# Mask, maximum and shift of a tile's attention scores: one vector operation each over 1024 elements of two PSUM banks instead of two of 512

## The reference, cut to what matters

```python
x = x + attn(cond(x, ...), W_attn, b_attn, W_proj, b_proj)
x = x + ffn(gru(cond_2048, x, W_ih, W_hh, b_ih, b_hh), weight, scale_weight, bias)

# inside attn: 32 heads of width 8, 32 tokens
scores = jnp.einsum('bhqd,bhkd->bhqk', q, k) / jnp.sqrt(jnp.float32(D))
scores = jnp.where(causal, scores, jnp.float32(MASKED_BIAS))
scores = scores + alibi * m
probs = jax.nn.softmax(scores, axis=-1)
attn = jnp.einsum('bhqk,bhkd->bhqd', probs, v)
```

## Time and profile before

| | us |
|---|---|
| median of 3 runs | 511.05 (510.9 to 513.89) |
| span of the profiled execution, first to last instruction | 509.6 |
| PE busy / PEld busy | 472.8 / 426.2 |
| DVE busy | 359.8 |
| ACT busy | 242.5 |
| POOL busy | 49.6 |
| attention, start-up included | about 0 to 318 |
| GRU and output | about 318 to 509.6 |

### The profile page before, as it was taken

How to read it: one execution, slowest core, us unless ns; L and a number is a source line. 1 busy time by engine, 2 the same in 40 slices (tenths; PEclk the granted TensorE clock), 3 DMA queues, 4 the chain that set the end, 5 groups by cost and what they waited for, 6 DMA issues and landing times.

```text
span 509.6 us, 14167 instructions
## 1 busy us (share of the span) xinstructions
PE 472.8 (93%) x5310; PEld 426.2 (84%) x5310; DVE 359.8 (71%) x1049; ACT 242.5 (48%) x584; POOL 49.6 (10%) x67
## 2 busy tenths in 40 slices
PE   8489899999999999999989887799999999999993
PEld 5258698888897888888878776799999999999993
DVE  3814789697897896987876786356666677676665
ACT  1252554746556648365566443434444444444441
POOL 7321201201203012012020000000000000000000
PEclk9969999999999999999999999989999999999998
DMA  8525543443544534444443420000000000100001
GB/s 304 205 59 148 151 115 84 146 117 109 149 103 118 153 94 144 113 113 106 99 109 76 113 67 1 1 1 30 34 21 21 21 21 21 39 23 21 22 21 41
DMA packets 81596, 42.45 MB, mean 83 GB/s; under 512 B 53792, under 2 KB 74400, under 8 KB 81568
## 3 DMA queue, kind: packets, MB, share of 16 engines
q1 hardware_dynamic: 81568, 42.07, 28.9%
HBM read 25.28 MB, written 16.78 MB: 83 GB/s over the span
## 4 chain that ended last, share of the span: by engine, by line
PE 69%; DVE 11%; ACT 5%; issue 5%; POOL 3%; POOLq 0%; DVEq 0%; ACTq 0%
PE ps_s L1071 7%; PE ps_t L1083 6%; PE ps_s L1234 6%; PE ps_t L1234 6%; PE ps_o L1234 6%; PE ps_a L1034 5%; PE ps_t L1212 5%; PE ps_a L1212 5%; PE ps_m L1212 4%; PE ps_s L1212 4%; PE ps_m L1112 4%; PE ps_a L1025 4%; DVE mx L761 3%; PE ps_a L1000 3%; POOL yT_r L432 3%
## 5 line engine op out<-in xcount | busy, mean ns | idle before, releaser
L1071 PE MATMUL ps_s<-kbd,qbd 128*128 128x128 f32 x512 | 65.7, 282 | 0.0
L515 ACT ACTIVATE sc<-sc 128x512 f32<-128x512 f32 x64 | 38.8, 628 | 53.7 <-DVE sc L765 53.7
L753 DVE COPY_PREDICATED masked<-kst,ps_s 128x512 f32<-128x512 int32 x64 | 46.7, 739 | 24.3 <-issue 19.9
L1071 PEld LDWEIGHTS ps_s<-kbd,qbd 128*128 128x128 f32 x512 | 62.9, 196 | 0.1
L1025 PE MATMUL ps_a<-yT_r,w_qkv_r 128*128 128x512 f32 x192 | 52.9, 420 | 2.6 <-ACT yT_r L478 1.5
L1025 PEld LDWEIGHTS ps_a<-yT_r,w_qkv_r 128*128 128x128 f32 x192 | 35.6, 196 | 14.3 <-POOL yT_r L432 4.9
L896 DVE SCALAR_TENSOR_TENSOR rg<-ps_o,vec,rg 128x128 f32<-128x128 f32 x64 | 19.5, 346 | 35.3 <-PE ps_o L1234 28.5
L765 DVE TENSOR_TENSOR sc<-masked,mx 128x512 f32<-128x512 f32 x64 | 41.0, 681 | 0.0
L761 DVE TENSOR_REDUCE mx<-masked 128x16 f32<-128x512 f32 x64 | 40.4, 671 | 0.0
L1083 PE MATMUL ps_t<-kst,sc 128*128 128x128 f32 x256 | 35.2, 277 | 4.6 <-ACT sc L515 4.6
L788 DVE SCALAR_TENSOR_TENSOR xf<-ps_m,b_out,xf 128x128 f32 (+1 forms) x64 | 24.9, 435 | 19.1 <-PE ps_m L1112 19.0
(11 more groups left out here) (105 smaller groups left out, 874.6 us busy)
## 6 DMA issues: line engine op xcount, KB each, us to landing
xf<-in_x_feat SPq DMA_DIRECT2D x8, 512.0 KB, 4.3
xg<-in_x_tok SPq DMA_DIRECT2D x8, 512.0 KB, 4.7
q_dram<-qn SPq DMA_DIRECT2D x16, 256.0 KB, 3.2
k_dram<-kn SPq DMA_DIRECT2D x16, 256.0 KB, 3.0
qbd<-q_dram SPq DMA_DIRECT2D x64, 64.0 KB, 2.3
kbd<-k_dram SPq DMA_DIRECT2D x64, 64.0 KB, 2.2
v_dram<-vn SPq DMA_DIRECT2D x16, 256.0 KB, 2.5
vbd<-v_dram SPq DMA_DIRECT2D x64, 64.0 KB, 1.9
```

What stands on the lines that cost most here:

```text
L515: nc.scalar.activation(part, part, ACT.Exp).then_inc(sc_exp, 1)
L753: nc.vector.copy_predicated(kept, keep.unsqueeze(1).to_broadcast([P, NH // 2, S]), ps_s[:, h * 512:(h + 1) * 512].rearrange("p (h k) -> p ...
L1071: last = nc.tensor.matmul(bank[:, q * P:(q + 1) * P], tile_q[:, i % TH, :], kbd[:, :, i // TH, h * HW + q, cols], start=True, stop=True)
```

## The change

Mask, maximum and shift are done by one instruction each over all 1024 elements. The semaphores `sc_out`, `sc_max` and `sc_sub` now count tiles, not halves. The mask waits until both halves of the scores are there. Both exponentials wait for the one shift. The scores of the next tile wait for the one mask. The exponentials, the score products and the transposes stay in halves.

```diff
             def softmax_exp(n, p):
+                act.wait_ge(sc_sub, n + 1)
                 for h in range(2):
-                    act.wait_ge(sc_sub, 2 * n + h + 1)
                     part = sc[:, p, h * 512:(h + 1) * 512]
                     nc.scalar.activation(part, part, ACT.Exp).then_inc(sc_exp, 1)
...
             def softmax_mask(n, p, first=False):
-                for h, kept, _, _ in halves(p):
-                    if not first:
-                        dve.wait_ge(sc_sub, 2 * n - 1 + h)
-
-                    dve.wait_ge(sc_mm, 2 * n + h + 1)
-                    nc.vector.memset(carrier[:, h:h + 1], 0.0)
-                    nc.vector.copy_predicated(kept, keep.unsqueeze(1).to_broadcast([P, NH // 2, S]),
-                                              ps_s[:, h * 512:(h + 1) * 512].rearrange("p (h k) -> p h k", k=S)
-                                              ).then_inc(sc_out, 1)
+                if not first:
+                    dve.wait_ge(sc_sub, n)
+                dve.wait_ge(sc_mm, 2 * n + 2)
+                nc.vector.memset(carrier[:, 0:1], 0.0)
+                nc.vector.copy_predicated(by_head, keep.unsqueeze(1).to_broadcast([P, NH, S]),
+                                          ps_s[:, :].rearrange("p (h k) -> p h k", k=S)).then_inc(sc_out, 1)
 
             def softmax_shift(n, p):
-                for h, kept, _, m in halves(p):
-                    dve.wait_ge(sc_out, 2 * n + h + 1)
-                    nc.vector.tensor_reduce(m, kept, axis=AX_X, op=ALU.max).then_inc(sc_max, 1)
-
-                for h, kept, shifted, m in halves(p):
-                    dve.wait_ge(sc_max, 2 * n + h + 1)
-                    nc.vector.tensor_tensor(shifted, kept, m.unsqueeze(2).to_broadcast([P, NH // 2, S]),
-                                            ALU.subtract).then_inc(sc_sub, 1)
+                dve.wait_ge(sc_out, n + 1)
+                nc.vector.tensor_reduce(mx[:, p, :], by_head, axis=AX_X, op=ALU.max).then_inc(sc_max, 1)
+                dve.wait_ge(sc_max, n + 1)
+                nc.vector.tensor_tensor(sc[:, p, :].rearrange("p (h k) -> p h k", k=S), by_head,
+                                        mx[:, p, :].unsqueeze(2).to_broadcast([P, NH, S]),
+                                        ALU.subtract).then_inc(sc_sub, 1)
...
             def scores(n, g, i, first=False):
                 pe.wait_ge(k_in[i // 2], HG * DMA * (g + 1))
                 pe.wait_ge(q_in[i // 2], TB * DMA * (g + 1))
+                if not first:
+                    pe.wait_ge(sc_out, n)
                 for h in range(2):
-                    if not first:
-                        pe.wait_ge(sc_out, 2 * n - 1 + h)
```

More of the change, by code:

```diff
@@ L736, in rest_of_weights @@
                                         ALU.subtract).then_inc(wqkv_lo, 1)
[L738 to L743, removed]
-            def softmax_mask(n, p, first=False):
-                for h, kept, _, _ in halves(p):
-                    if not first:
-                        dve.wait_ge(sc_sub, 2 * n - 1 + h)
-                    dve.wait_ge(sc_mm, 2 * n + h + 1)
-                    nc.vector.memset(carrier[:, h:h + 1], 0.0)
-                    nc.vector.copy_predicated(kept, keep.unsqueeze(1).to_broadcast([P, NH // 2, S]),
-                                              ps_s[:, h * 512:(h + 1) * 512].rearrange("p (h k) -> p h k", k=S)
-                                              ).then_inc(sc_out, 1)
@@ L757, in softmax_shift @@
-            def softmax_shift(n, p):
-                for h, kept, _, m in halves(p):
-                    dve.wait_ge(sc_out, 2 * n + h + 1)
-                    nc.vector.tensor_reduce(m, kept, axis=AX_X, op=ALU.max).then_inc(sc_max, 1)
-                for h, kept, shifted, m in halves(p):
-                    dve.wait_ge(sc_max, 2 * n + h + 1)
-                    nc.vector.tensor_tensor(shifted, kept, m.unsqueeze(2).to_broadcast([P, NH // 2, S]),
-                                            ALU.subtract).then_inc(sc_sub, 1)
+            by_head = masked[:, :].rearrange("p (h k) -> p h k", k=S)
```

## The result

The changed kernel takes 540.88 us (540.53 to 541.61, 4 runs) where the kernel before takes 512.29 (510.9 to 513.89): a ratio of 1.0559 with a 95% interval of 1.0532 to 1.0585, slower. The forecast was 537.5, range 526 to 548. The forecast stood on a median of 511.05 for the kernel before, whose four runs lie at 510.9, 511.05, 513.53 and 513.89. On the profiled executions the span went from 509.6 to 538.9, by 29.3 us (28.6 between the medians); the sum in the prediction was 26.4.

A forecast was written before the change was run, and what follows sets the result against it. PE sets the pace, so what matters is when DVE's results reach it. First tile 1.3, six groups 20.2, group 6 3.6 and group 7 1.3 sum to 26.4 us on a median of 511.05: 537.5 us, range 526 to 548.

The forecast's parts named there:

- The operations: On DVE, mask, maximum and shift of 1024 elements take 1.27, 1.20 and 1.21 us, extrapolated from a 768-element subtraction.
- the rival of dearer operations: Each merged DVE operation costs twice a row of 512; about 10 us more, 548 us; chance 0.08.
- The dependent starts: On DVE, an instruction waiting for its neighbour starts 0.03 after its end instead of overlapping by 0.07: 0.10 each.
- The chain: From one tile's scores through mask, maximum and shift: first exponential 1.25 us later, shift and `on` 0.65 later.
- Step 0 and step 1: In each group, late exponentials on ACT's queue delay `oT` and so PE's projection: 1.14 us each.
- Step 2: In each group, PE has 6 us of other products covering the delay: cost 0, about 0.7 us of cover left.
- Step 3: In each group, PE already waits for the first exponential, which moves with the transposes by 1.09 us.
- its rival of less cost: ACT does not hold the projection; steps 0 and 1 cost 0.45 us each, 528 us in all; chance 0.12.
- The sign that it named: PE idle for `oT` ahead of the projection in steps 0 and 1, some 0.4 us in the record.
- PE's busy time: In the profile of the change, PE's busy time stays as before.
- The clock: Rival: more waits give PE the lower clock for a tenth of its attention time; 24 us more, about 560; chance 0.03.
- The rival on the other side: DVE sets the pace and fewer operations save 0.27 us in each of 32 tiles: 8.6 us, 502 us; chance 0.02.

The follow-up runs named there:

- e5: The kernel before with only the maximum merged into one operation of 1024, mask and shift staying in halves: 517.35 us, 1.0088 of before.
- e6: The change with `attn_out` placed ahead of the first q or k chunk on ACT in steps 0 and 1: 536.44 us, 1.0458 of before.
- the fillers: The change with unread products into unused PSUM where PE waits in groups 5 to 7: 538.83 us, on another chip 538.72 us.
- the repeated change: The change itself, unaltered, run again on the same chip as its filled version: 540.27 us, 1.0541 of before.
- e2, e3: Not numbered in the text; by its one shift, either shift alone merged (525.09 us) or the change with mask back in halves (525.82 us).
- e1: Not numbered in the text; by its separate shifts, the kernel before with only the mask merged, maximum and shift in halves: 529.54 us, 1.0322 of before.

## Why the prediction was right, step by step

**The operations.** Expected 1.27, 1.20 and 1.21 us; measured 1.33, 1.22 and 1.22. The slope from the 768 subtraction held for the shift to 0.01. The mask was under-priced by 0.06: 512 elements more cost it 0.59, not 0.53. The bound above, twice the row of 512, was far off, and so the rival of dearer operations (548 us) is out. The Trainium skill's formula for an fp32 tensor_tensor ("VectorE: DVE Perf Modes", the section on the TRN2 errata) gives 1.224 us for the shift; the trace agrees, with a mean of 1224 ns.

**The dependent starts.** Expected 0.03 to 0.04 after the end; measured 0.04 between mask and maximum (184.84 to 184.88) and 0.03 between maximum and shift (186.10 to 186.13). e5, which makes one merge that costs nothing but such starts, is 0.9% slower, by 5 us. The Trainium skill ("VectorE: DVE Perf Modes", the section on the DRAIN) says that the semaphore between neighbours costs nothing extra. Here it does not hold: two independent shifts of 0.68 us span 1.28, so they overlap by 0.07 to 0.08, and the dependent ones above start 0.03 to 0.04 after the end.

**The chain.** The exponential was to start 3.84 us behind the end of the scores, and starts after 3.93; `on` to end after 4.5, and ends after 4.62. At least half of each error is the mask's 0.06; the rest is maximum and shift, each a little over what was expected. They did not reach the projection, since the two exponentials, both released by the one shift, take 1.15 and not the 1.23 that the prediction kept. The projection was to start 8.18 behind the start of the scores, and does.

**The steps.** Step 0 and step 1 were to cost 1.14 each; from scores to scores they cost 1.15 and 1.16. Step 2, costed at nothing, takes 9.88 us from scores to scores (190.59 to 200.47) for 9.89. Step 3 was to cost 1.09 and costs 0.96 (200.47 to 209.83, 9.36 for 8.40): the first exponential is 1.08 later, but the eight transposes behind it take 1.10 instead of 1.26. The group of 37.6 is the 37.7 forecast.

**The reason given in steps 0 and 1** was only a part of it. The sum came out by the way through ACT's queue, which is the last of two to end. The prediction treated it as the only one: its rival of less cost let these steps fall to 0.45 if ACT did not hold the projection. e6 took ACT's part away and 0.74 stayed, because `on` is late too. The arithmetic had the number (0.65 for `on`) but never asked what PE does while it waits for it. The rival's 528 would not have come true on its condition; 536 did. So the number for these steps was right because the prediction followed the later of two ways; that there was a second one just ahead of it, it did not see. The sign that it named, some 0.4 us of idle time for `oT`, is 0.39 in the weight loads of step 1, but PE's own idle time is for `on`, 0.57 in step 0 and 0.80 in step 1, and over the whole kernel 13.0 us more than before.

**PE's busy time** was to be as before and rose by 7.7 us. In groups 0 to 4, at clock 1.00, it is 172.35 us for 168.86, 0.7 a group; a part of it is that a row which has waited no longer overlaps the row ahead of it, as with the projection's 1.16 for 1.06, which the prediction had priced. The three last groups have 4.6 more, with the long rows of the lower clock in them.

**The three last groups** hold 2.5 of the 2.9 us that the sum missed. The step that failed is "The clock", a rival with 24 us and chance 0.03, argued from one stretch at clock 1.00 in which PE is idle for 26% of the time (22% from 278 to 350 in the change). It came true in a size that I had not written: the loop of five groups keeps its full clock with 8% of idle time, but in the three last groups the clock falls to the lower level in some stretches of a few us. With the fillers it did not fall in these groups (clock 1.00 from 278 to 350 in both profiled executions), their lengths came near those forecast, and beside the change on one chip the kernel came down by 1.5 us. So the lower clock is what the sum missed there, and filling PE's waits is what kept it away in these executions. It is not shown that idle time alone decides: group 7 of the repeated change kept 1.00 without fillers, and the kernel before keeps it through the same groups. Why the same sequence of instructions fell at different places in two executions is open.

**The rival on the other side**, that DVE sets the pace and fewer operations win: DVE did get 3.4 us less busy time, two fifths of the 8.6, and it bought nothing: the idle time ahead of the masks rose from 24.3 to 44.0 us.

## What to carry to other kernels

When an operation is cut in halves at a PSUM bank, look at who uses the first half early before merging: here the halves let DVE start beside PE and ACT beside DVE, worth 15 to 17 us and 13 us, while all that the merging could save was 0.15 us a tile, under 5 us in all. DVE, with idle time ahead of the merged operation, gained nothing from fewer instructions, and PE and ACT on either side paid. Cost each of the ways by which a delay reaches the pacing engine; the last one gives the sum, but the next one, here 0.4 us behind, is what stays when the last is mended.

## What the runs showed of the hardware that was not expected

- The predicated copy from PSUM costs 739 ns for 512 elements and 1326 for 1024: 1.15 ns for each further element, more than the 1.06 of the maximum (671 and 1216) and the shift (681 and 1224).
- The pair of exponentials of step 1 starts 0.03 to 0.04 us behind its release either way, but lasts 1.15 us when both are released by one shift (change, e2, e3), and 1.23 when the second waits for a shift of its own (before, e1).
- Eight products that start behind a wait have a row of 1.16 us, without a wait 1.06 (the projection in the change and in e6).
- In the change the granted clock stayed at 1.00 from 62 to 278 us, with PE idle 8% of the time, and fell to the lower level (0.50 from 282 to 286 in one execution) for some us between 278 and 350, at places that differ between executions of one kernel; with products of no use in PE's waits it was 1.00 there in two executions.
